# Quantised attention with keys on partitions, four heads in column groups, GpSimd rounding, and output written in parts

## The chip, the cores and the metric

The kernel runs on one core of a Trainium2 chip. The metric is device microseconds of one execution, and of several executions the median. A core has TensorE (PE in the rows; PEld is its weight load), VectorE (DVE), ScalarE (ACT), GpSimd (POOL), and the queue engine SP, which here issues nearly all transfers. They run side by side and wait for each other through semaphores. SBUF is the working memory of 128 partitions; PSUM has eight banks of 512 float32 columns by 128 partitions and takes TensorE's results.

## What is computed

The reference is four gated layers of cross-attention and feed-forward on x of shape (4, 512, 512), so 2048 rows of 512. The change lies in the attention of layer 1, over all 2048 rows as queries and all 2048 rows of the context as keys, with 16 heads of 32:

```
q = fq(LN(x) @ Wq + bq) per head and row;  k = fq(ctx @ Wk + bk) likewise   # fq: 8 bits, symmetric
v = fq(ctx @ Wv + bv) per column
s = q k^T / sqrt(32);  p = exp(s - max s)
p255 = round(255 p)            # 0 to 255
o = (p255 @ v) / sum(255 p)    # per head
x = x + tanh(g) * (o @ Wp + bp)
```

The mask of this layer leaves every key in.

## The kernel before

The program is a list of stages, one after the other, with a barrier of all engines between them. Each stage has its own semaphores and one instruction list for each engine. Layer 1's attention consists of split_weights, quantised_heads for the keys, quantised_values, split_weights, transposed_parts (which normalises x and turns it), quantised_heads for the queries, attention_quantised, split_weights of the output weights, transposed_parts of the attention's output, and project_and_add. A number "in parts" is stored as two float16 values, high and low, so that TensorE can multiply float32 data in float16 steps: in PARTS, high by high, low by high, high by low.

quantised_heads works on 16 tiles of 128 rows. TensorE projects a tile, VectorE adds the bias, takes each head's largest magnitude, scales and rounds, and TensorE turns the result, so that the head's 32 numbers lie on partitions. For the keys (L = 2) it multiplies the rounded numbers by their step again, and ScalarE and GpSimd split them in two parts. For the queries (L = 1) the rounded integers are turned as they are, and the steps go to sq, one for each row and head.

attention_quantised has queries on partitions. It works in 256 tiles: for each head, 16 tiles of 128 queries against all 2048 keys. A tile n goes through these steps:

- score_for_top: four products of 512 keys, of which VectorE takes the maximum each (L1616); top_of and shift_of make of them the shift of the exponential. This runs two tiles ahead.
- score: the same four products again into two pairs of banks, and ScalarE takes the exponential of each pair of banks (1024 keys, L1585), with the row's shift as bias and sq as scale. The result is written as int16, which rounds it, and the unrounded sum goes to z.
- turn: 16 transposes of 128x128 (L1516) bring keys to partitions. VectorE copies one half back as float16 (L1629), ScalarE the other (L1591).
- mix: 16 products of 128x128 by 128x32 (L1524), and VectorE moves the 32 columns to o (L1634).
- At a head's end GpSimd divides by the sums (L1495 to L1497).

The order is written out by hand in each engine's list (tile, head_from_tile_1). SP loads the queries and keys of head h + 3 into a ring of three once head h is scored. After the stage, transposed_parts splits o into high and low, turns it into oT, and project_and_add multiplies it.

Two other attentions of the program, attention_clipped (layer 2) and attention_causal (layer 3), already have keys on partitions, take the sums by a product with ones, and put four float32 products of 32 columns side by side in TensorE's column groups. Some rows below are theirs.

## Time and profile before

| | |
|---|---|
| median of 3 runs | 3445.23 us (3444.49 to 3451.05) |
| the profiled execution's own time | 3446.79 us |
| its span | 3445.1 us |
| TensorE busy | 2739.6 us, 80% |
| VectorE busy | 2552.2 us, 74% |
| ScalarE busy | 1874.1 us, 54% |
| GpSimd busy | 706.1 us, 20% |
| mean granted clock of TensorE | 0.897 of full speed |

The shares are means over all stages, which have different limits. Layer 1's attention_quantised begins at 872.95 us and ends at 1798.71 us, more than a quarter of the span. A busy time does not say what an engine waited for; that is read from the timeline, which lists each instruction, or each run of alike ones, with its start and its time.

### The profile page before, as it was taken

To read this page: it belongs to the slowest core of one execution; us is meant where nothing else is said; L and a number is where in the kernel's file an instruction comes from. 1 tells how busy PE (TensorE), PEld (TensorE's weight loads), DVE (VectorE), ACT (ScalarE), POOL (GpSimd) and SP (SyncE) were. 2 spreads that over 40 slices of the span, in tenths; PEclk is the share of its full clock that TensorE was granted. 3 is DMA by queue.
4 is the path that set the end of the run, shared out by engine and by line. 5 is a ranking of instruction groups with operands and counts; after the bars stand their busy time and mean duration, and the time that the engine had idled before them with its cause. 6 is when DMAs were issued, how large, how long until landed. Compare 5 with 4: busy or idle time off the path is not lost. (4 is left out here: it accounts for less than half of the span.)

```text
span 3445.1 us, 63421 instructions
## 1 busy us (share of the span) xinstructions
PE 2739.6 (80%) x21404; PEld 1417.0 (41%) x21404; DVE 2552.2 (74%) x4757; ACT 1874.1 (54%) x2709; POOL 706.1 (20%) x602
## 2 busy tenths in 40 slices
PE   5768999677799999999977777777797657759983
PEld 3344444233465656565644333334111323224542
DVE  5656677657899999999975666434798878986547
ACT  2564433232699999999982533313676313434541
POOL 4340000102110100101004233203012603550013
PEclk8978999887899999999999888887998869978996
DMA  4533421200100000000001000100431100022301
GB/s 150 182 127 123 147 74 37 83 0 16 25 7 13 7 13 7 13 7 13 1 13 63 26 0 0 61 15 13 98 74 37 59 0 0 0 83 50 66 8 52
DMA packets 65334, 151.93 MB, mean 44 GB/s; under 512 B 11840, under 2 KB 20048, under 8 KB 63376
## 3 DMA queue, kind: packets, MB, share of 16 engines
q1 hardware_dynamic: 62368, 140.43, 13.6%
q0 software_dynamic: 2800, 9.18, 0.8%
q8 instruction: 117, 1.92, 0.2%
q14 instruction: 49, 0.40, 0.0%
HBM read 93.61 MB, written 24.38 MB: 34 GB/s over the span
## 5 line engine op out<-in xcount | busy, mean ns | idle before, releaser
L1616 DVE TENSOR_REDUCE s_top<-ps 128x1 f32<-128x512 f32 x1024 | 656.2, 682 | 30.4 <-PE ps L1511 30.1
L1585 ACT ACTIVATE s_prob<-ps,s_shift,m_sq 128x1024 int16<-128x1024 f32 x512 | 615.3, 1202 | 30.9 <-DVE s_shift L1624 30.9
L1511 PE MATMUL ps<-s_ks,s_qs 128*128 128x512 f16 x1024 | 352.6, 386 | 61.7 <-issue 15.0
L1516 PEld LDWEIGHTS ps<-ident,s_prob 128*128 128x128 f16 x4096 | 272.7, 98 | 123.4 <-DVE m_o L1634 52.2
L1516 PE MATMUL ps<-ident,s_prob 128*128 128x128 f16 x4096 | 314.1, 220 | 0.7 <-ACT s_prob L1585 0.5
L1504 PE MATMUL ps<-s_ks,s_qs 128*128 128x512 f16 x1024 | 307.2, 382 | 0.8 <-ACT s_prob L1585 0.5
L1591 ACT ACTIVATE s_probT<-ps 128x1024 f16<-128x1024 int16 x256 | 262.1, 1024 | 6.2 <-PE ps L1516 5.8
L1007 PE MATMUL ps<-m_hT,m_w 128*128 128x512 f16 x1024 | 231.9, 381 | 1.8 <-PEq L104 1.8
L248 PE MATMUL ps<-ident,s_parts 128*128 128x128 f16 x640 | 76.4, 293 | 129.1 <-POOL s_parts L239 127.3
L1629 DVE CAST s_probT<-ps 128x1024 f16<-128x1024 int16 x256 | 174.0, 680 | 5.0 <-PE ps L1516 5.0
L2288 DVE TENSOR_SCALAR s_prob<-ps,s_cap 128x1024 f32<-128x1024 f32 x128 | 158.1, 1269 | 25.2 <-PE ps L2197 25.2
L1495 POOL TENSOR_TENSOR s_sums<-s_z 128x16 f32<-128x16 f32 x16 | 3.5, 218 | 835.3 <-DVE m_o L1634 835.3
L2897 DVE TENSOR_REDUCE s_ntop<-ps 128x1 f32<-128x512 f32 (+3 forms) x256 | 107.3, 482 | 86.6 <-PE ps L2757 86.6
L2232 ACT ACTIVATE s_prob<-s_prob 128x1024 f32<-128x1024 f32 x128 | 131.1, 1051 | 58.8 <-DVE s_prob L2288 55.8
L1058 ACT ACTIVATE s_silu<-ps,scale 128x512 f32<-128x512 f32 x64 | 43.9, 686 | 205.4 <-PE ps L1007 205.4
L1007 PEld LDWEIGHTS ps<-m_hT,m_w 128*128 128x128 f16 x1024 | 100.5, 98 | 124.0 <-issue 2.4
L1511 PEld LDWEIGHTS ps<-s_ks,s_qs 128*128 (+1 forms) x1024 | 80.1, 96 | 168.4 <-DVE s_top L1616 108.7
L2211 PE MATMUL ps<-s_prob,m_values 128*32 128x512 f32 x512 | 136.0, 610 | 12.8 <-ACT s_prob L2232 12.6
L1524 PE MATMUL ps<-s_hv,s_probT 128*128 128x32 f16 x4096 | 142.4, 177 | 1.7 <-ACT s_probT L1591 1.7
L2868 ACT ACTIVATE s_prob<-ps 128x384 f32<-128x384 f32 (+1 forms) x192 | 89.7, 516 | 88.2 <-PE ps L2780 87.9
L2214 PE MATMUL ps<-s_prob,s_ones 128*32 128x512 f32 x512 | 136.0, 610 | 0.0
L1524 PEld LDWEIGHTS ps<-s_hv,s_probT 128*128 128x128 f16 x4096 | 129.7, 96 | 2.2 <-issue 2.2
(402 smaller groups left out, 5844.3 us busy)
## 6 DMA issues: line engine op xcount, KB each, us to landing
s_qs<-m_qT SPq DMA_DIRECT2D x144, 128.0 KB, 3.1
s_ks<-m_kT SPq DMA_DIRECT2D x96, 128.0 KB
numbers<-s_numbers SPq DMA_DIRECT2D x21, 512.0 KB, 2.8
s_slabs<-numbers SPq DMA_DIRECT2D x21, 512.0 KB, 6.0
m_ks<-context_parts SPq DMA_DIRECT2D x12, 512.0 KB
expert_rows<-s_y SPq DMA_DIRECT2D x19, 256.0 KB, 2.0
s_rows_in<-in_ctx SPq DMA_DIRECT2D x16, 256.0 KB, 3.1
x_sb<-in_L_ffn_W_up SPq DMA_DIRECT2D x4, 1024.0 KB, 6.7
```

The lines of the kernel that those rows point to most:

```text
L1007: i = pe.matmul(k.ps[:, 2 * (n % 2) + j, :], wt[:, c, cols(n, P)], hT[:, l, c, cols(g, GT)], start=(l == c == 0), stop=(l == 1 and c == DC ...
L1504: j = pe.matmul(pair(half)[:, m, :], qs[:, hb, bass.ds(t * P, P)], ks[:, hb, cols(2 * half + m, 512)], start=True, stop=True)
L1511: pe.matmul(quarter_at(q), qs[:, hb, bass.ds(t * P, P)], ks[:, hb, cols(q, 512)], start=True, stop=True).then_inc(s.top_scored, 1)
L1516: j = pe.transpose(turned(half, F16)[:, cols(m, P)], prob[:, u, cols(8 * half + m, P)].bitcast(F16), k.ident[:])
L1524: j = pe.matmul(output, probT[:, u, m, :], hv[:, hb, m, :], start=(m == 0), stop=(m == T - 1))
L1585: act.activation(prob[:, u, cols(half, HALF)], pair(half).rearrange("p m n -> p (m n)"), ACT.Exp, bias=shift[:, u:u + 1], scale=sq[:, bass ...
L1591: act.activation(probT[:, u, 8:16, :].rearrange("p m n -> p (m n)"), turned(1, I16), ACT.Copy).then_inc(s.half1_copied, 1)
L1616: dve.tensor_reduce(top4[:, u, q:q + 1], quarter_at(q), AX.X, ALU.max).then_inc(s.top_read, 1)
L1629: dve.tensor_copy(probT[:, u, 0:8, :].rearrange("p m n -> p (m n)"), turned(0, I16)).then_inc(s.half0_copied, 1)
L2211: pe.matmul(values_at(m)[cols(j, HD), :], values[:, b * KT + t, 2 * pair + j, :], prob[:, n % R, j, :], start=(t == 0), stop=(t == KT - 1))
L2214: i = pe.matmul(sums_at(m)[cols(j, HD), :], ones[:], prob[:, n % R, j, :], start=(t == 0), stop=(t == KT - 1))
L2288: dve.tensor_scalar(prob[:, n % R, :, :], k.ps[:, 2 * (n % A):2 * (n % A) + 2, :], cap[:, tile:tile + 1], -LIMIT, ALU.min, ALU.max).then_i ...
```

## The change

attention_quantised is written anew, with keys on partitions. It works in 16 blocks of four heads (the four of one 128-partition group) by 512 queries; a block has 16 steps n, one for each tile of 128 keys.

- The queries come as two parts, already multiplied by their steps, as the keys do: quantised_heads is called with parts=qT, and sq is gone. Queries and keys are stacked three times in 96 rows (high by high, high by low, low by high), so a score is one product of 96 rows.
- top: as before, four products of 512 keys with 128 queries on partitions, and VectorE takes their maxima, now negated. It runs AHEAD = 19 steps ahead of the scores. Once a block, shifts makes of them 128x16 values in three float16 parts (five small instructions), turn_shift transposes these, copy_shift brings them to SBUF, and SP writes them to three further rows of the queries, rows 96 to 98, against which the keys have a constant in the same rows. The product of 99 rows then gives the score with the shift taken off.
- score: four products a step (one for each head) of 128 keys by 512 queries, in a ring of three banks. ScalarE takes the exponential of each bank by itself, as float32, with ln 255 as bias.
- GpSimd rounds the step's 128x2048 numbers into float16 integers (one instruction).
- mix_values, two steps late (LAG): four products of 32 columns, one for each head, in four column groups of one bank, integers by values in float16. mix_ones: the same with the unrounded float32 numbers and ones, for the sums, in another bank. Both accumulate over 16 steps.
- Once a block: ScalarE evacuates both banks (step 1 of the next block), pick_sums brings the sums' rows to partitions (step 5), VectorE inverts them, spread_inverse lays the inverses out (step 8), VectorE divides, ScalarE writes the high part, GpSimd the low part, straight into qT. project_and_add reads qT; the transposed_parts of the output is gone.
- In quantised_heads, the multiplication by scale is fused into the one by the inverse step.

The order of TensorE in a step is score 0, top 0, mix_values, score 1, top 1, mix_ones, score 2, top 2, score 3, top 3. The whole stage is written out without loops.

```diff
 def quantised_heads(k, src, w, bias, scale, sq=None, ints=None, parts=None, context=False):
...
-                    if scale != 1.0:
-                        v.done(dve.tensor_scalar(inv[:], inv[:], scale, None, ALU.mult))
-                    v.done(dve.tensor_tensor(scaled[:, u, :].rearrange("p (h d) -> p h d", d=HD),
-                                             rows[:, u, :].rearrange("p (h d) -> p h d", d=HD),
-                                             inv[:].unsqueeze(2).broadcast_to([P, H, HD]), ALU.mult))
+                    v.done(dve.scalar_tensor_tensor(scaled[:, u, :].rearrange("p (h d) -> p h d", d=HD),
+                                                    rows[:, u, :].rearrange("p (h d) -> p h d", d=HD), scale,
+                                                    inv[:].unsqueeze(2).broadcast_to([P, H, HD]), ALU.mult, ALU.mult))
...
-def attention_quantised(k, qT, sq, kT, values, o):
+def attention_quantised(k, qT, kT, values):
...
+            for b in range(BLOCKS):
+                sp.wait_ge(s.top_read, number["shift", b] + 1)
+                sp.dma_start(qs[ROWS:ROWS + 3, b % 3, :, :], shiftT[:, b % 2, :]).then_inc(shifted[b % 3], 16)
+                if b and b + 2 < BLOCKS:
+                    sp.wait_ge(s.scored, A * KT * b)
+                    for a in range(A):
+                        queries(b + 2, a, q_loaded[(b + 2) % 3])
+                if b and b % G == 0 and b // G + 1 < DC:
+                    for a in range(A):
+                        keys(b // G + 1, a, k_loaded[(b // G + 1) % 2])
...
+            for n in range(STEPS + KT):
+                if n < STEPS:
+                    pool.wait_ge(s.exp_ready, A * (n + 1))
+                    if n >= 3:
+                        pool.wait_ge(s.mixed, n - 2)
+                    pool.tensor_scalar(ints[:, n % 3, :, :], prob[:, n % 4, :, :], ROUND, ROUND, ALU.add,
+                                       ALU.subtract).then_inc(s.rounded, 1)
+                if n >= KT and n % KT == LOW:
+                    b = n // KT - 1
+                    at = (slice(None), 1, b // G, cols(b % G, GT))
+                    pool.wait_ge(s.hi_ready, b + 1)
+                    pool.tensor_tensor(qT[at], num[:], qT[:, 0, b // G, cols(b % G, GT)], ALU.subtract).then_inc(s.lo_ready, 1)
...
+            def bank_free(job):
+                if job >= 3:
+                    pe.wait_ge(s.top_read, job - 2)
...
+            def score(n, a):
+                b, t = n // KT, n % KT
+                g = A * n + a
+                if t == a == 0:
+                    pe.wait_ge(shifted[b % 3], 16 * (b // 3 + 1))
+                if g >= 3:
+                    pe.wait_ge(s.exp_ready, g - 2)
+                pe.matmul(score_at(g), ks[0:ROWS + 3, b // G % 2, a, cols(t, P)], qs[0:ROWS + 3, b % 3, a, :],
+                          start=True, stop=True).then_inc(s.scored, 1)
+
+            def mix_values(n):
+                b, t = n // KT, n % KT
+                if t == 0 and b:
+                    pe.wait_ge(s.evacuated, 2 * b)
+                pe.wait_ge(s.rounded, n + 1)
+                for a in range(A):
+                    pe.matmul(mixed_at[cols(a, HD), :], values[:, t, cols(b // G * A + a, HD)], ints[:, n % 3, a, :],
+                              start=(t == 0), stop=(t == KT - 1))
+
+            def mix_ones(n):
+                t = n % KT
+                for a in range(A):
+                    j = pe.matmul(sums_at[cols(a, HD), :], ones[:], prob[:, n % 4, a, :],
+                                  start=(t == 0), stop=(t == KT - 1))
                 j.then_inc(s.mixed, 1)
...
+            def pick_sums(b):
+                job = number["pick", b]
+                bank_free(job)
+                pe.wait_ge(s.evacuated, 2 * (b + 1))
+                for q in range(TG):
+                    j = pe.matmul(top_at(job)[:, cols(q, A)], sums[:, cols(q, P)], pick[:], start=True, stop=True)
+                j.then_inc(s.top_scored, 1)
+
+            def spread_inverse(b):
+                job = number["wide", b]
+                bank_free(job)
+                pe.wait_ge(s.top_read, number["pick", b] + 1)
+                for q in range(TG):
+                    for a in range(A):
+                        j = pe.matmul(top_at(job)[cols(a, HD), cols(q, P)],
+                                      inv[:, A * q + a:A * q + a + 1].broadcast_to([P, HD]), k.ident32[:],
+                                      start=True, stop=True)
+                j.then_inc(s.top_scored, 1)
+
+            for m in range(-AHEAD, END):
+                i = m + AHEAD
+                for a in range(A):
+                    if 0 <= m + 1 < STEPS:
...
+                        score(m + 1, a)
+                    if i < STEPS:
+                        top(i, a)
+                    if a == 0 and LAG <= m < STEPS + LAG:
+                        mix_values(m - LAG)
+                    if a == 1 and LAG <= m < STEPS + LAG:
+                        mix_ones(m - LAG)
+                if i % TILES == 0 and 0 < i <= STEPS:
+                    turn_shift(i // TILES - 1)
+                if m >= KT and m % KT == PICK:
+                    pick_sums(m // KT - 1)
+                if m >= KT and m % KT == WIDE:
+                    spread_inverse(m // KT - 1)
...
+            def exp(n, a):
+                g = A * n + a
+                if a == 0 and n >= 4:
+                    act.wait_ge(s.mixed, n - 3)
+                act.wait_ge(s.scored, g + 1)
+                act.activation(prob[:, n % 4, a, :], score_at(g), ACT.Exp, bias=ln255[:, 0:1]).then_inc(s.exp_ready, 1)
+
+            def evacuate(b):
+                if b:
+                    act.wait_ge(s.lo_ready, b)
+                act.wait_ge(s.mixed, KT * (b + 1))
+                act.activation(sums[:], sums_at, ACT.Copy).then_inc(s.evacuated, 1)
+                act.activation(num[:], mixed_at, ACT.Copy).then_inc(s.evacuated, 1)
...
+            def shifts(b):
+                dve.wait_ge(s.top_read, number["top", TILES * (b + 1) - 1, 3] + 1)
+                hi, mid, lo = (shift[:, b % 2, r, :] for r in range(3))
+                v.done(dve.tensor_reduce(least[:], ntop[:, b % 2, :, :], AX.X, ALU.min))
+                v.done(dve.tensor_scalar(hi, least[:], 1.0 / SIXTEEN, None, ALU.mult))
+                v.done(dve.scalar_tensor_tensor(rest[:], least[:], 1.0 / SIXTEEN, hi, ALU.mult, ALU.subtract))
+                v.done(dve.tensor_scalar(mid, rest[:], 1.0, None, ALU.mult))
+                dve.tensor_tensor(lo, rest[:], mid, ALU.subtract).then_inc(s.shift_ready, 1)
...
 def layer1_xattn(k):
...
-            quantised_heads(k, hT, wq, k.i.L1_xattn_bq, scale, sq=sq[:].rearrange("p (h t) -> p t h", t=T), ints=qT)
-        o = sb("o", [P, H, T, HD], F32)
-        attention_quantised(k, qT, sq, kT, values, o)
+            quantised_heads(k, hT, wq, k.i.L1_xattn_bq, scale, parts=qT)
+        attention_quantised(k, qT, kT, values)
...
-            transposed_parts(k, oT, tiles=o)
-            project_and_add(k, oT, wp, k.i.L1_xattn_bp, 1)
+            project_and_add(k, qT, wp, k.i.L1_xattn_bp, 1)
```

## Rows read from the trace of the kernel before

**Rows 1.** The page's costliest groups: the attention's maxima, exponentials and copies.

```profile
L1616 DVE TENSOR_REDUCE s_top<-ps 128x1 f32<-128x512 f32 x1024 | 656.2, 682 | 30.4 <-PE ps L1511 30.1
L1585 ACT ACTIVATE s_prob<-ps,s_shift,m_sq 128x1024 int16<-128x1024 f32 x512 | 615.3, 1202 | 30.9 <-DVE s_shift L1624 30.9
...
L1591 ACT ACTIVATE s_probT<-ps 128x1024 f16<-128x1024 int16 x256 | 262.1, 1024 | 6.2 <-PE ps L1516 5.8
```

**Rows 2.** Busy time by stretch: PE, PEld, DVE, ACT, POOL, then PE clock, DMA, GB/s.

```profile
896.00:1792.00 896.00, 846.83 (x10180) 542.42 (x10178) 865.98 (x2028) 875.57 (x1272) 71.16 (x59) 0.99 0.04 8
```

**Rows 3.** Timeline at the attention's ends: start us, us, engine, line, operation, count.

```profile
872.95 0.62 SPq L1473 DMA_DIRECT2D s_qs<-m_qT  x1
...
889.16 2.48 DVE L1616 TENSOR_REDUCE s_top<-ps 128x1 f32<-128x512 f32 x4 [1.00 <-PE ps L1511]
...
1797.66 1.05 POOL L1497 TENSOR_TENSOR m_o<-m_o,s_sums 128x512 f32<-128x512 f32 x1
...
1810.63 0.69 DVE L1216 TENSOR_TENSOR m_wp<-s_nat,m_wp 128x512 f16<-128x512 f32 x1 [0.58 <-ACT m_wp L1210]
...
1831.59 0.69 DVE L267 COPY m_oT<-ps 128x1024 f16<-128x1024 f16 x1 [0.41 <-PE ps L248]
```

**Rows 4.** Timeline of TensorE: a plain run, then a group in columns.

```profile
295.27 3.62 PE L1007 MATMUL ps<-m_hT,m_w 128*128 128x512 f16 x16
...
2499.78 0.38 PE L2197 MATMUL ps<-s_qs,s_ks 128*128 128x512 f16 x1
...
2500.09 0.62 PE L2211 MATMUL ps<-s_prob,m_values 128*32 128x512 f32 x2
...
2500.55 0.60 PE L2211 MATMUL ps<-s_prob,m_values 128*32 128x512 f32 x2
...
2501.09 0.60 PE L2197 MATMUL ps<-s_qs,s_ks 128*128 128x512 f16 x2
```

**Rows 5.** Timeline of the causal attention: picking of sums, exponentials, evacuation.

```profile
3155.06 1.00 PE L2802 MATMUL ps<-s_pick,s_sums 128*128 128x4 f32 x8
...
3199.85 0.57 ACT L2868 ACTIVATE s_prob<-ps 128x512 f32<-128x512 f32 x1
...
3204.65 0.59 ACT L2876 ACTIVATE s_sums<-ps 64x512 f32<-64x512 f32 x1 [0.23 <-PE ps L2791]
...
3205.92 1.05 ACT L2868 ACTIVATE s_prob<-ps 128x512 f32<-128x512 f32 x2
```

**Rows 6.** Groups of GpSimd by shape: busy us, mean ns of one, idle before.

```profile
L2273 POOL TENSOR_TENSOR s_out<-s_num,s_inv 128x512 f32<-128x512 f32 x16 | 20.3, 1270 | 126.2 <-DVE s_inv L2296 126.2
...
L1487 POOL COPY s_hv<-m_values 128x512 f16<-128x512 f16 x16 | 9.7, 611 | 1.0
...
L1495 POOL TENSOR_TENSOR s_sums<-s_z 128x16 f32<-128x16 f32 x16 | 3.5, 218 | 835.3 <-DVE m_o L1634 835.3
...
L141 POOL CAST ident<-ident 128x128 f16<-128x128 f32 x1 | 0.3, 291 | 0.1
```

**Rows 7.** The page's DMA issues: KB of one, median us from issue to landing.

```profile
s_qs<-m_qT SPq DMA_DIRECT2D x144, 128.0 KB, 3.1
```

**Rows 8.** Timeline of quantised_heads: of the keys, then of the queries.

```profile
643.85 4.44 PE L1246 MATMUL ps<-m_wkv,m_cT 128*128 128x512 f16 x13 [21.86 <-PEq L104]
...
707.07 1.15 POOL L1318 TENSOR_TENSOR s_f<-s_rows,s_f 128x512 f16<-128x512 f32 x1 [2.97 <-ACT s_f L1330]
707.68 0.57 DVE L1290 TENSOR_SCALAR s_step<-s_amax 128x16 f32<-128x16 f32 x1
...
717.59 1.02 ACT L1339 ACTIVATE m_kT<-ps 128x1024 f16<-128x1024 f16 x1 [1.44 <-PE ps L1254]
...
811.08 8.12 PE L1246 MATMUL ps<-m_wq,m_hT 128*128 128x512 f16 x30 [1.69 <-PEq L104]
...
816.79 0.17 DVE L1290 TENSOR_SCALAR s_step<-s_amax 128x16 f32<-128x16 f32 x1
...
871.63 0.60 ACT L1335 ACTIVATE m_qT<-ps 128x512 f16<-128x512 f16 x1 [3.00 <-PE ps L1254]
```

335 lines of the change are left out of this document (142 added, 193 removed).

## The prediction

> **What bounds the kernel now.** I first read the page's costliest groups [rows 1] to find where the touched function stands, then the busy times of its long stretch [rows 2], then the timeline at its two ends [rows 3]. From 896 to 1792 us ScalarE is busy 875.6 of 896 us (98%), VectorE 97%, TensorE 95% and GpSimd 8%. Why ScalarE: each of the 256 tiles (16 heads by 16 query tiles) asks it for two exponentials of 1202 ns and one copy of 1024 ns, 3.43 us [rows 1], and 256 of these are 878 us. VectorE is just behind with four maxima and a copy. The reader should see that three engines are nearly full: relief for one only hands the end to the next. The stage starts with SP's first transfer at 872.95 and ends with GpSimd's product at 1798.71 [rows 3]: 925.8 us. All other stages stand before or behind it, so the sum is over stages, each with its own bound.
>
> **The new step.** There are again 256 steps (16 blocks of four heads by 512 queries, 16 key tiles each). A step has on TensorE four score and four top products of 512 columns, a group of four value products in float16 and a group of four ones products in float32. On ScalarE four exponentials, on VectorE four maxima, on GpSimd one rounding of 128x2048.
>
> TensorE. A 512-column product costs 0.216: sixteen take 3.62, less one duration 0.38, by 15 [rows 4]. Eight are 1.73. The ones group is priced by the attention that already packs four float32 products in column groups of 32: the last plain product starts at 2499.78, the group at 2500.09, its second passes at 2500.55, the next plain product at 2501.09 [rows 4]. That is 1.31 us from plain to plain, less the 0.216 of the plain one: 1.10, of which two passes are 0.92 and about 0.18 is going in (0.09) and out (0.08). The trace has no float16 group in columns. Bounds: 0.22, if one pass is all it costs, and 0.86, if its four products follow each other. I take one pass (0.216), the 0.04 by which four starts are staggered, and the same in and out, 0.44, since the float32 rows show both. Step: 1.73 + 1.10 + 0.44 = 3.27 us.
>
> The Trainium skill, TensorEngine Tiling (Array Packing), Key Properties, says that changing the tiling mode drains TensorE; the float32 rows agree with 0.09 in and 0.08 out. This speaks against the change, because the order of the step changes mode four times; without that rule's cost the step would be about 2.9 us, the first rival below.
>
> VectorE. Four maxima take 2.48 back to back, the last one's tail included [rows 3]: 0.60 apart, 2.40 a step. ScalarE. Two exponentials of 128x512 take 1.05, each 0.57: 0.48 apart [rows 5], 1.92 a step. Both lie beside TensorE's 3.27. I checked the rings by these numbers: the score three back has been read some 0.5 us or more before its bank is wanted, and the top three back likewise.
>
> GpSimd. No row shows this rounding. One-input rows: 128 columns cost 291 ns, 512 cost 611 [rows 6], so 0.83 ns a column, and 2048 are 1.9 us. Two-input rows: 16 columns 218 ns, 512 columns 1270, so 2.12 ns, and 2048 are 4.5 us. The rounding has one input and two constants, so I take 1.9, hidden under 3.27; 4.5 is kept for the range. It has two steps of slack before the value products need it. The Trainium skill, GPSIMD Engine Reference, Elementwise, side-by-side cycle accounting, puts a body of up to two operations at 1.03 cycles an element, an estimated 1.8 us, but also names about 1.8 cycles as a best case, an estimated 3.1; no row here tells them apart.
>
> **Sum over the new stage.**
> - Start: six transfers issued at 0.62 each before the first top [rows 3], a landing of 3.1 [rows 7], the first product: 7.5.
> - Lead-in: tops run 19 steps ahead, and the value products start two steps late, so 21 steps go at VectorE's 2.40: 50.4, plus the first shift chain of 1.5 (five small dependent instructions, 0.3 each): 51.9. TensorE may fall to 1.2 GHz here; its four products would be 1.7, still under 2.40. This is new: before, tops were two tiles ahead.
> - 235 full steps at 3.27: 768.5.
> - The last 18 steps have no tops: 4 x 0.216 + 1.10 + 0.44 = 2.40, 43.2, with one block's extra 3.6; then three steps of 1.53: 51.4.
> - Tail: two copies (1.2), pick (0.95), reciprocal, spread (1.1), division, high part, low part (1.2): about 7.2.
> - Once a block on the path, 14 times inside the full steps: pick_sums, eight instructions in 1.00, of which 0.95 hold the next [rows 5]; spread_inverse, 16 float32 products of 128 columns four at a time, 4 x 2 x 0.11 + 0.18 = 1.1; and the evacuation. ScalarE waits for the block's last ones group, ending 2.5 us into the step, with the next four exponentials queued behind the wait. The two copies (0.59 each [rows 5]) put the first of these at 3.65; its bank is wanted for the fourth score at 2.84 and is free at about 4.45 (0.57 of the exponential, and an estimated 0.2 to the release): a stall of 1.6. Together 3.65 x 14 = 51.
> - The shift chain, 15 times. VectorE's own slack is 0.87 a step. But GpSimd rounds while it runs, and a small VectorE instruction between SBUF tiles waits for a GpSimd instruction: 0.57 us under GpSimd's product, 0.17 without it [rows 8]. The rounding runs from about 0.7 to 2.65 of a step and the chain starts at 1.05, so it is held to 2.65 and ends near 3.8. The next four maxima wait behind it, and TensorE, three banks ahead, waits for the first of them: 1.9, plus 0.1 for the shift's transpose, 2.0 x 15 = 30. Bounds: 0.4 if nothing holds it, 8 if each of its four such instructions waits a whole rounding.
>
> Sum: 7.5 + 51.9 + 768.5 + 51.4 + 7.2 + 51 + 30 = 967.5 against 925.8: +41.7.
>
> **Transfers.** The queue SP issues twelve query transfers a block (7.5 us) and waits for scores. By the order written out, the next queries have 14 steps (45 us) and the shift rows two steps (6.5 us, 4.8 in the lead-in) against an issue of 0.62 and a landing of about 3. I cost them at nothing; without that cover a late shift is some 2 us a block.
>
> **The stages around it.** The queries' quantised_heads now writes two parts, as the keys' does: keys 643.85 to 718.61, queries 811.08 to 872.23 [rows 8], 74.8 against 61.2, so +13.6. The fused multiplication changes nothing for the keys, whose scale is 1. Dropping the transposed_parts of the output takes its stage away, from 1811.32 to 1832.28 [rows 3]: -21.0. Total: 41.7 + 13.6 - 21.0 = +34.3. The profiled execution took 3446.79, 1.6 above the median of 3445.23, so the forecast is 3481.1 for such an execution and 3480 for a median. Measurement can tell 0.2% (6.9 us) from no change.
>
> **Rivals.**
> - Faster: the changes of mode cost nothing and the float16 group one pass. Step 1.73 + 0.22 + 0.92 = 2.87; 253 steps by 0.40 are 101 us: 3379. For it: no row shows a float16 group, and weight loads elsewhere hide under products. Against: 2500.09 and 2501.09. It decides once the step is under 3.27 - 41.2/253 = 3.11; a half-way case lands at 3430. Chance 0.20.
> - GpSimd takes about 3.2 us, half-way between its two rates. The low part (1.2 a block) is no longer hidden, the last 18 steps go at 3.3 instead of 2.4, and the chain is held longer: 17 + 16 + 15, 3530. Chance 0.15. The Trainium skill's 1.8 cycles on the page named above would be this case.
> - GpSimd at the two-input rate: 256 x 4.6 + 16 x 1.2 + 65 = 1262, +336 in the stage: 3774. Chance 0.05. It decides above 3.3 us a rounding.
> - The locks take the full 8 us a block: 6 x 15 = 90 more: 3570. Chance 0.08.
> - The forecast, TensorE bound near 3.27 with stalls of 2 to 6 us a block: 0.52, its own range 3443 to 3510.
>
> Faster takes the first rival and a sliver of the forecast's low side, 0.22; within 0.2% another 0.12 of that low side, where the evacuation and the chain hide; slower the rest, 0.66. The range 3425 to 3560 reaches into the first rival and over the second and leaves out about 0.2.
>
> **What would show it.** TensorE near full in the stage at 3.27 us a step, VectorE near 75%, ScalarE near 60%, GpSimd near 60%; a rounding of 1.9 us; 0.44 between plain products around the float16 group; one gap of 1.6 us a block waiting for an exponential and one of about 2 for a maximum; 45 us of maxima alone at the start; the queries' stage 13 us longer, the output's 21 us gone. Wrong would be: a step under 3.11, or GpSimd as the releaser of the value products.

## The result, and the profile after

The changed kernel takes 4413.09 us (median of four, 4412.75 to 4417.90), against 3444.86 for the kernel before beside it: a ratio of 1.2815, with a 95% interval of 1.2799 to 1.2831. It is 968 us slower. The forecast was 3480, with a range to 3560: the direction was right and the size was not.

The page's costliest groups of the changed kernel (busy us, mean ns of one, then the idle time before them and what ended it); they answer to [rows 1]:

```profile
L1519 POOL TENSOR_SCALAR s_ints<-s_prob 128x2048 f16<-128x2048 f32 x256 | 1808.8, 7087 | 56.8 <-ACT s_prob L1628 56.8
L1660 DVE TENSOR_REDUCE s_ntop<-ps 128x1 f32<-128x512 f32 x1024 | 669.0, 687 | 867.9 <-PE ps L1544 865.6
L1628 ACT ACTIVATE s_prob<-ps,s_ln 128x512 f32<-128x512 f32 x1024 | 665.0, 687 | 1084.4 <-PE ps L1561 1082.1
...
L1570 PE MATMUL ps<-s_ints,m_values 128*32 128x512 f16 x1024 | 129.6, 496 | 443.1 <-POOL s_ints L1519 443.1
```

One group stands out. GpSimd's rounding takes 7.087 us, 256 times, and has no idle time but the lead-in's 56.8 us. The value products have waited 443 us, all of it for that rounding: the sign that the forecast named last, GpSimd as their releaser. The busy times of a long stretch say the same (us, then PE, PEld, DVE, ACT, POOL, PE clock, DMA share, GB/s), to be held against [rows 2]:

```profile
1000.00:1700.00 700.00, 486.70 (x2219) 112.25 (x2216) 341.55 (x441) 265.14 (x411) 700.00 (x105) 0.72 0.03 6
```

GpSimd is busy 700.00 of 700 us, no other engine more than 70%. TensorE's granted clock is 0.72 here, against 0.99 in [rows 2]. The timeline at the stage's two ends, to be held against [rows 3]:

```profile
887.31 2.67 SPq L1478 DMA_DIRECT2D s_qs<-m_qT  x3
...
2776.95 0.62 PE L1570 MATMUL ps<-s_ints,m_values 128*32 128x512 f16 x4 [4.74 <-POOL s_ints L1519]
...
2786.35 1.15 POOL L1525 TENSOR_TENSOR m_qT<-s_num,m_qT 128x512 f16<-128x512 f32 x1 [9.45 <-ACT m_qT L1639]
...
2799.88 0.33 SPq L1711 DMA_DIRECT2D s_bias_bc<-in_L_xattn_bp  x1
```

The stage runs from 887.31 to 2787.50, 1900.2 us against 925.8: +974.4. It begins 14.4 us later than before, for the queries' longer stage. After the output's weights the projection follows at once, so the stage of transposed parts with its 21.0 us is gone. Together +967.8, against 971.1 between the two profiled spans (4416.2 and 3445.1). The stage is told in one line: 55.4 to the first rounding (942.75), 256 roundings 7.07 apart (1810), fifteen low parts of 1.16 between them in the same queue (17.4), some 7 of gaps, and 10.6 behind the last rounding, which ends at 2776.9 (the sixteenth low part is in it).

Two side effects stand in the timeline of the middle:

```profile
1470.02 49.47 POOL L1519 TENSOR_SCALAR s_ints<-s_prob 128x2048 f16<-128x2048 f32 x7
...
1477.17 0.62 PE L1570 MATMUL ps<-s_ints,m_values 128*32 128x512 f16 x4 [3.42 <-POOL s_ints L1519]
...
1484.24 4.44 DVE L1668 SCALAR_TENSOR_TENSOR s_rest<-s_least,s_shift 128x16 f32<-128x16 f32 x1
...
1488.71 2.56 DVE L1669 TENSOR_SCALAR s_shift<-s_rest 128x16 f16<-128x16 f32 x1
...
1496.40 0.61 PE L1544 MATMUL ps<-s_ks,s_qs 96*128 96x512 f16 x1 [9.48 <-DVE s_ntop L1660]
```

TensorE waits 3.42 us for the rounding, and its next group of four takes 0.62 instead of 0.40, at the lower of its two clocks (1.2 GHz). VectorE's small instructions of 128x16, 0.17 us where nothing holds them, take 4.44 and 2.56, because a rounding holds them. The roundings start 7.07 apart, at 1477.09, 1484.16 and 1491.23. The first of the two, with two tensors as input, comes free 4.5 us into a rounding and not at its end; the second, with one, starts there and is held to the end. The chain of the shift takes over 12 us this way, and TensorE waits 9.48 for a maximum behind it. This costs nothing here, since GpSimd never runs dry of work meanwhile.

### The profile page after: what moved, and what is told of

Same layout as the page of the kernel before. It is cut to its first block and busy times, and to the rows that moved or that the text cites. A ratio compares the mean times of both kernels' runs of the same rounds, so it can differ in the third digit from the quotient of the medians.

```text
span 4416.2 us, 48145 instructions
## 1 busy us (share of the span) xinstructions
PE 3163.0 (72%) x16876; PEld 1160.9 (26%) x16876; DVE 2568.3 (58%) x3829; ACT 1687.2 (38%) x2501; POOL 2454.1 (56%) x812
## 3 DMA queue, kind: packets, MB, share of 16 engines
q8 instruction: 117, 1.92, 0.2%
## 5 line engine op out<-in xcount | busy, mean ns | idle before, releaser
L1519 POOL TENSOR_SCALAR s_ints<-s_prob 128x2048 f16<-128x2048 f32 x256 | 1808.8, 7087 | 56.8 <-ACT s_prob L1628 56.8
L1660 DVE TENSOR_REDUCE s_ntop<-ps 128x1 f32<-128x512 f32 x1024 | 669.0, 687 | 867.9 <-PE ps L1544 865.6
L1628 ACT ACTIVATE s_prob<-ps,s_ln 128x512 f32<-128x512 f32 x1024 | 665.0, 687 | 1084.4 <-PE ps L1561 1082.1
L1544 PE MATMUL ps<-s_ks,s_qs 96*128 96x512 f16 x1024 | 503.7, 494 | 134.2 <-DVE s_ntop L1660 125.7
L1561 PE MATMUL ps<-s_qs,s_ks 99*128 99x512 f16 x1024 | 497.5, 491 | 16.1 <-ACT s_prob L1628 15.0
L1570 PE MATMUL ps<-s_ints,m_values 128*32 128x512 f16 x1024 | 129.6, 496 | 443.1 <-POOL s_ints L1519 443.1
L1576 PE MATMUL ps<-s_prob,s_ones 128*32 128x512 f32 x2048 | 422.3, 911 | 0.0
L1561 PEld LDWEIGHTS ps<-s_qs,s_ks 99*128 99x128 f16 x1024 | 112.7, 111 | 558.7 <-issue 407.5
L1544 PEld LDWEIGHTS ps<-s_ks,s_qs 96*128 96x128 f16 x1024 | 113.9, 111 | 256.9 <-DVE s_ntop L1660 172.3
L2629 POOL TENSOR_TENSOR s_summed<-s_y,s_bits 128x512 f32<-128x512 f32 x64 | 104.2, 1629 | 71.3 <-DVE s_bits L2659 71.3
L2249 PE MATMUL ps<-s_prob,s_ones 128*32 128x512 f32 x512 | 135.2, 607 | 0.0
```

The costliest lines, as they stand in the source:

```text
L1519: pool.tensor_scalar(ints[:, n % 3, :, :], prob[:, n % 4, :, :], ROUND, ROUND, ALU.add, ALU.subtract).then_inc(s.rounded, 1)
L1544: pe.matmul(top_at(job), qs[0:ROWS, b % 3, a, cols(tile, P)], ks[0:ROWS, c % 2, a, cols(q, GT)], start=True, stop=True).then_inc(s.top_sco ...
L1561: pe.matmul(score_at(g), ks[0:ROWS + 3, b // G % 2, a, cols(t, P)], qs[0:ROWS + 3, b % 3, a, :], start=True, stop=True).then_inc(s.scored, 1)
L1570: pe.matmul(mixed_at[cols(a, HD), :], values[:, t, cols(b // G * A + a, HD)], ints[:, n % 3, a, :], start=(t == 0), stop=(t == KT - 1))
L1576: j = pe.matmul(sums_at[cols(a, HD), :], ones[:], prob[:, n % 4, a, :], start=(t == 0), stop=(t == KT - 1))
L1628: act.activation(prob[:, n % 4, a, :], score_at(g), ACT.Exp, bias=ln255[:, 0:1]).then_inc(s.exp_ready, 1)
```

## The experiments

Each starts from the changed kernel. Times are medians, ratios are against the kernel before on the same chip.

**1. GpSimd's operations by themselves.** A stage of its own, ahead of the attention, runs each operation three times, each waiting for the one before:

```diff
+    v.done(pool.tensor_scalar(b16[:], a32[:], ROUND, ROUND, ALU.add, ALU.subtract))      # L1434
+    v.done(pool.tensor_scalar(b16[:, 0:512], a32[:, 0:512], ROUND, ROUND, ALU.add, ALU.subtract))
+    v.done(pool.tensor_scalar(b16[:], a32[:], 1536.0, None, ALU.add))
+    v.done(pool.tensor_scalar(b32[:], a32[:], ROUND, ROUND, ALU.add, ALU.subtract))
+    v.done(pool.tensor_copy(b16[:], a32[:]))
+    v.done(pool.tensor_tensor(b32[:], a32[:], a32[:], ALU.add))
+    v.done(pool.tensor_scalar(b16[:], a16[:], ROUND, ROUND, ALU.add, ALU.subtract))      # L1446
```

The rounding was then repeated beside a busy VectorE (maxima, then roundings) and a busy ScalarE, and at last VectorE's own forms were run alone.

> The changed kernel with a stage of its own ahead of the attention, in which single operations run one after the other, each waiting for the one before; output unchanged. In the changed kernel GpSimd's rounding (two operations, float32 to float16, 128x2048) took 7.09 us, against 1.9 in the forecast. Theory A: that is GpSimd's own rate for this form, so it takes about 7.0 us (3.4 ns a column) with all other engines idle, and no less with VectorE or ScalarE busy beside it; 512 columns then take about 1.9. Theory B: contention (memory ports shared with VectorE, or with all) makes it slow: alone it takes 2 to 4.5 us, and 7 only beside a busy VectorE. Theory C: each arithmetic operation costs: the form with one operation takes about half, 3.5. Theory D: the float16 output costs: float32 to float32 is far below 7. The same operation on VectorE is expected at 1.2 us for float32 input (the nearest row of the kernel before has 1.23 for 128x2048) and 0.6 to 1.2 for float16 input.

The groups of that stage by shape (busy us, mean ns of one, idle before):

```profile
L1434 POOL TENSOR_SCALAR s_b<-s_a 128x2048 f16<-128x2048 f32 x3 | 21.3, 7102 | 0.3
L1440 POOL TENSOR_SCALAR s_b<-s_a 128x2048 f32<-128x2048 f32 x3 | 21.3, 7087 | 0.2
L1446 POOL TENSOR_SCALAR s_b<-s_a 128x2048 f16<-128x2048 f16 x3 | 21.3, 7085 | 0.3
L1438 POOL TENSOR_SCALAR s_b<-s_a 128x2048 f16<-128x2048 f32 x3 | 16.1, 5365 | 0.2
L1444 POOL TENSOR_TENSOR s_b<-s_a 128x2048 f32<-128x2048 f32 x3 | 10.8, 3597 | 0.2
...
L1436 POOL TENSOR_SCALAR s_b<-s_a 128x512 f16<-128x512 f32 x3 | 5.8, 1922 | 0.2
L1442 POOL CAST s_b<-s_a 128x2048 f16<-128x2048 f32 x3 | 5.7, 1891 | 0.2
```

With every other engine idle the rounding takes 7.10 us. It is GpSimd's own rate for this form, 3.46 ns a column, whatever the types. Theory A holds; B (contention) and D (the float16 output) fall. C is half right: with one operation instead of two it takes 5.37, three quarters and not half. A plain copy of the same 2048 columns takes 1.89, and an addition of two tensors 3.60. So the forecast's 1.9 us was the right price for a copy, and not for a copy with arithmetic: an operation with a constant costs 3.5 us over the copy, and the second one 1.7 more.

The same line beside busy engines, and VectorE's rounding beside it (durations are min/median/max):

```profile
L1450 POOL TENSOR_SCALAR s_b<-s_a x9: 7085/7086/8063, 990.2 to 1055.3; 128x2048 f16<-128x2048 f32 x9
```

```profile
L1464 DVE TENSOR_SCALAR s_c<-s_a x12: 1226/1227/7989, 1039.0 to 1073.1; 128x2048 f16<-128x2048 f32 x12
```

Maxima or ScalarE's copies beside it change nothing (7.09). VectorE's rounding does collide: alone 1.23 us, beside GpSimd's up to 7.99, since one waits for the other. The three VectorE roundings of 7.98 to 7.99 each end 1.1 us behind GpSimd's instruction, and GpSimd's three beside them take 7.93 to 8.06 instead of 7.09. The Trainium skill, SBUF — State Buffer, "SBUF: two separate sides", states an exclusive lock on the pair of ports for a whole instruction. The 7.99 agree with it. The 4.44 above don't: there a small instruction came free 4.5 us into a rounding of 7.09, so it is not always the whole instruction. From float16, VectorE's rounding takes 0.69.

**2. A quarter of the rounding.**

```diff
-  pool.tensor_scalar(ints[:, n % 3, :, :], prob[:, n % 4, :, :], ROUND, ROUND, ...
+  pool.tensor_scalar(ints[:, n % 3, 0, :], prob[:, n % 4, 0, :], ROUND, ROUND, ...
...
-  pe.matmul(mixed_at[cols(a, HD), :], values[:, t, cols(b // G * A + a, HD)], ints[:, n % 3, a, :],
+  pe.matmul(mixed_at[cols(a, HD), :], values[:, t, cols(b // G * A + a, HD)], ints[:, n % 3, 0, :],
```

> GpSimd rounds only the first of the four heads (128x512), and the value products of all four read that one tile: three quarters of the rounding are left out, all other work stays. Theory (the forecast with one wrong price): a rounding costs by its columns, 7.09 / 4 = 1.8 us, GpSimd leaves the path, TensorE bounds at 3.27 us a step and the time is the forecast's, 3480 (3440 to 3510). Rival 1: the 7 us are mostly a fixed cost or contention, the rounding stays above 3.3 and the time above 3550. Rival 2: the forecast's other terms were also too low (mode changes, evacuation, shift chain, the clock), then 3520 to 3600 with a rounding of 1.8. Rival 3: mode changes cost less than 0.18 a group: below 3440.

It took 3477.06 us, a ratio of 1.0096 (1.0079 to 1.0112). The forecast for the whole change was 3480. With the rounding at the price that the forecast gave it, the rest of the sum comes out. Its stage, from the timeline:

```profile
883.21 2.84 SPq L1478 DMA_DIRECT2D s_qs<-m_qT  x3
...
1849.05 1.15 POOL L1525 TENSOR_TENSOR m_qT<-s_num,m_qT 128x512 f16<-128x512 f32 x1 [7.98 <-ACT m_qT L1639]
```

That is 967.0 us, where the sum said 967.5. How much of that is luck is seen in its steps:

```profile
1092.83 1.92 POOL L1519 TENSOR_SCALAR s_ints<-s_prob 128x512 f16<-128x512 f32 x1 [1.35 <-ACT s_prob L1628]
...
1093.51 0.17 DVE L1668 SCALAR_TENSOR_TENSOR s_rest<-s_least,s_shift 128x16 f32<-128x16 f32 x1
...
1166.38 0.39 PE L1561 MATMUL ps<-s_qs,s_ks 99*128 99x512 f16 x1 [1.30 <-ACT s_prob L1628]
...
1168.37 1.93 PE L1576 MATMUL ps<-s_prob,s_ones 128*32 128x512 f32 x8
...
1175.66 0.40 PE L1570 MATMUL ps<-s_ints,m_values 128*32 128x512 f16 x4
1175.99 0.39 PE L1561 MATMUL ps<-s_qs,s_ks 99*128 99x512 f16 x1
1176.22 0.38 PE L1544 MATMUL ps<-s_ks,s_qs 96*128 96x512 f16 x1
1176.53 1.06 PE L1576 MATMUL ps<-s_prob,s_ones 128*32 128x512 f32 x8
1177.53 0.39 PE L1561 MATMUL ps<-s_qs,s_ks 99*128 99x512 f16 x1
...
1178.94 0.40 PE L1570 MATMUL ps<-s_ints,m_values 128*32 128x512 f16 x4
```

From values group to values group are 3.28 us, against 3.27 in the sum. The stall for the evacuation is 1.30, and the whole step with it is 4.88 us, 1.6 over a plain one, as in the sum. Behind it the clock falls for one ones group (1.93 instead of 1.06) and four products; blocks in which it does so are 58.08 us apart, those without it 56.50. The chain of the shift costs TensorE 0.5 (that step is 3.80), where the sum had 2.0. Its four small arithmetic instructions stood inside a running rounding of 1.92 us, as the sum had it, and still took 0.17 to 0.19 each: none was held. So the block's 57.97 was right as a whole with two wrong parts: 2.0 for a lock that held nothing here, and nothing for a clock that cost 1.6.

**3. Half of the rounding**, the first edit above with `0:2` for `0`; the value products read `ints[:, n % 3, a % 2, :]`.

> GpSimd rounds two of the four heads (128x1024); the value products of the other two read the same tiles: half of the rounding is left out. Theory (GpSimd bounds once a rounding is over 3.3 us): by the rows of 512 columns (1.92) and 2048 (7.09) it takes 3.65; 256 x 3.66 + 58 lead-in + 16 x 1.16 for the low parts + 10 tail = 1024 in the stage, 98 more than before, less 7 around it: 3536 (3520 to 3560). Rival: TensorE's own step and stalls at a lower clock add to it, since it now waits for GpSimd in every step: 3600 and more.

3511.12 us, 1.0199 (1.0182 to 1.0216), 9 below the range given. A rounding takes 3.63, as expected. GpSimd is busy without a gap and TensorE nearly so, as the busy times show (columns as above):

```profile
1000.00:1600.00 600.00, 571.16 (x3684) 159.90 (x3688) 436.08 (x735) 421.72 (x687) 600.00 (x174) 0.99 0.05 13
```

The two engines' blocks are nearly equal: blocks are 58.64 us apart, GpSimd's full queue, where TensorE alone took 56.50 or 58.08 in run 2. The forecast's "decides above 3.3 us" compared GpSimd with a bare step; with the block's own stalls in TensorE's account it decides above (56.5 - 1.16) / 16 = 3.46 or (58.1 - 1.16) / 16 = 3.56, an estimate from run 2's two kinds of block.

**4. VectorE rounds**, all four heads, behind its maxima.

```diff
+            def round(n):
+                dve.wait_ge(s.exp_ready, A * (n + 1))
+                if n >= 3:
+                    dve.wait_ge(s.mixed, n - 2)
+                dve.tensor_scalar(ints[:, n % 3, :, :], prob[:, n % 4, :, :], ROUND, ROUND, ALU.add,
+                                  ALU.subtract).then_inc(s.rounded, 1)
...
                 if i < STEPS:
                     tops(i)
+                if 0 <= m < STEPS:
+                    round(m)
```

> All work is done, but the rounding moves from GpSimd to VectorE, behind the four maxima of its step. Theory: VectorE takes 2.40 + 1.23 = 3.63 us a step and becomes the bound, 235 steps of 3.63 instead of 3.27, no lock on the shift chain, some 2 us of small VectorE instructions a block on the path: 3515 (3490 to 3550). Rival 1: the rounding on VectorE is as slow as on GpSimd, 7 us: above 4900. Rival 2: VectorE gets it at half the columns' time (0.7 us), then TensorE bounds and it is 3450 to 3480.

3531.0 us, 1.0255 (1.0238 to 1.0272), within the range. VectorE is the bound at 3.52 us a step (1193.51 to 1197.03; 3.8 on a block's mean), the rounding 1.22:

```profile
1193.51 1.22 DVE L1677 TENSOR_SCALAR s_ints<-s_prob 128x2048 f16<-128x2048 f32 x1
1194.64 2.47 DVE L1654 TENSOR_REDUCE s_ntop<-ps 128x1 f32<-128x512 f32 x4
1197.03 1.22 DVE L1677 TENSOR_SCALAR s_ints<-s_prob 128x2048 f16<-128x2048 f32 x1
```

Moving one operation to another engine wins back 882 of the 968 us, with all the work done.

**5. GpSimd copies instead of computing.** The copy converts to int16, and this conversion stands in for the rounding; no run compares its integers one by one with those of the two operations. TensorE reads the bits of the integer n as the float16 n x 2^-24.

```diff
-        ints = s.sb("ints", [P, 3, A, GT], F16)
+        ints = s.sb("ints", [P, 3, A, GT], I16)
...
-  pool.tensor_scalar(ints[:, n % 3, :, :], prob[:, n % 4, :, :], ROUND, ROUND, ALU.add, ALU.subtract)
+  pool.tensor_copy(ints[:, n % 3, :, :], prob[:, n % 4, :, :])
...
-  pe.matmul(mixed_at[...], values[...], ints[:, n % 3, a, :], ...
+  pe.matmul(mixed_at[...], values[...], ints[:, n % 3, a, :].bitcast(F16), ...
...
-  act.activation(num[:], mixed_at, ACT.Copy)
+  act.activation(num[:], mixed_at, ACT.Copy, scale=float(2 ** 24))
```

> All work is done, but GpSimd no longer adds and subtracts the rounding constant: it copies the float32 probabilities to int16, whose conversion rounds, and the value products read the integers' bits as float16, where n is n times 2 to the minus 24; the evacuation of the values multiplies by 2 to the 24. By the measurement alone a GpSimd copy of 128x2048 takes 1.89 us, against 7.1 for the two operations. Theory (only the price of the rounding was wrong): the step is TensorE's 3.27 us and the time that of the kernel which rounds a quarter, 3477 (3465 to 3490). Rival 1: the conversion to int16 is not at the copy's rate and GpSimd bounds again: above 3600. Rival 2: TensorE is slower on such bits: 3500 and more.

3491.33 us, 1.0142 (1.0125 to 1.0159), one above its range. The copy takes 1.893 us in place:

```profile
L1519 POOL CAST s_ints<-s_prob 128x2048 int16<-128x2048 f32 x191 | 361.6, 1893 | 328.9 <-ACT s_prob L1627 328.9
```

Most of the 14 us over the run with a quarter of the rounding are TensorE's waits for a maximum behind the shift chain, 0.86 us in each block (from 1000 to 1700 us: us in total, times, longest):

```profile
PE ps L1560 <- ACT s_prob L1627: 14.4, 11, 1.3
PE ps L1543 <- DVE s_ntop L1659: 10.3, 12, 0.9
```

The copy, unlike run 2's rounding, holds the chain's first small instruction to its own end: 1.46 us instead of 0.17, in every block. This is the whole change with only the price of the rounding put right: it still isn't faster than the kernel before.

**6. Both column groups together**, with a quarter of the rounding, as in run 2.

```diff
-                    if a == 1 and LAG <= m < STEPS + LAG:
+                    if a == 0 and LAG <= m < STEPS + LAG:
                         mix_ones(m - LAG)
```

> GpSimd rounds a quarter (three quarters of the rounding are left out), as in the first timed run, and the ones group follows the values group at once instead of two plain products later, so that TensorE goes into column groups and out of them once a step and not twice. Theory of the forecast: going in and out costs 0.18 each time, 253 x 0.18 = 45 less: 3432 (3420 to 3445). Rival 1: changes of mode are free and the group's time is its own: 3477. Rival 2: with both groups together the score ring stalls (1.5 us without a score, ScalarE has two banks in hand), so that the gain is lost: 3460 to 3500.

3406.56 us, 0.9897 (0.9881 to 0.9914), better than its range: 70 less than run 2, where 45 were expected. The step, from one values group to the next:

```profile
1122.06 0.40 PE L1570 MATMUL ps<-s_ints,m_values 128*32 128x512 f16 x4
1122.29 1.03 PE L1576 MATMUL ps<-s_prob,s_ones 128*32 128x512 f32 x8
1123.25 0.39 PE L1561 MATMUL ps<-s_qs,s_ks 99*128 99x512 f16 x1
...
1125.10 0.40 PE L1570 MATMUL ps<-s_ints,m_values 128*32 128x512 f16 x4
```

3.04 us instead of 3.28: one way out of the column groups and one way in, 0.24. Times 253 that is 61, an estimate. Counted by blocks, they are 52.94 apart against 56.50 in run 2 where its clock stays up: 3.6 less, with a shorter stall at the evacuation (0.87 instead of 1.30, as the ones are done sooner) and somewhat longer steps around the shift. The 1.6 of low clock that eleven of run 2's blocks had besides are gone: the clock is 1.00 from 950 to 1750 us. 15 x 3.6 + 11 x 1.6 = 71. The Trainium skill, TensorEngine Tiling (Array Packing), Key Properties, says that a change of the tiling mode drains TensorE; the 0.24 agree with it.

**7. Runs 5 and 6 together**, all work done, sums from unrounded float32.

> All work is done: GpSimd copies to int16, probabilities and ones stay float32, and the ones group follows the values group at once. Theory: the order saves what it saved with a quarter of the rounding (3477 to 3407, 70), so the run with the copy to int16, 3491, becomes 3421 (3410 to 3435), 0.7% under the kernel before. Rival: the longer GpSimd instruction and VectorE's shift chain behind it cost the gain: 3445 or more.

3430.62 us, 0.9970 (0.9959 to 0.9980): within its range, 0.3% faster than the kernel before. The small instruction of the shift chain is held again (L1666 took 1.44 us in the blocks read, 0.17 where nothing holds it), and TensorE waits 1.24 for a maximum behind it.

**8. Float16 probabilities and ones**, added to run 5, so that the ones group is one pass.

```diff
-        prob = s.sb("prob", [P, 4, A, GT], F32)
+        prob = s.sb("prob", [P, 4, A, GT], F16)
...
-        ones = s.sb("ones", [P, HD], F32)
+        ones = s.sb("ones", [P, HD], F16)
```

> As the run with the copy to int16, and the probabilities and the ones are float16 (the sums are then of probabilities rounded to float16), so that the ones group is one pass. Theory: TensorE's step is 1.73 + 0.44 + 0.44 = 2.61 us, 0.66 less on 235 steps and on the last 18, 167 less than 3477, and with VectorE only 0.2 below TensorE its small instructions cost some 15 more: 3325 (3300 to 3350). Rival 1: a float16 group in columns costs near the float32 one when it reads float16 written by ScalarE, no gain: 3470. Rival 2: VectorE or the evacuation bounds at 2.9 or more a step: 3390 and more.

3510.39 us, 1.0191 (1.0126 to 1.0257). Its executions scatter more than any other's, from 3489.58 to 3553.12, the longer the lower their mean clock; the profiled one took 3492.92. So it is no faster than run 5, and whether it is slower is open. None of the three mechanisms explains it. Where TensorE has its full clock the step is 2.61 us, as the theory said (1403.06 to 1405.67). But its mean clock is 0.77:

```profile
1000.00:1600.00 600.00, 570.47 (x2972) 165.72 (x2970) 449.36 (x721) 421.09 (x671) 314.47 (x171) 0.77 0.05 13
```

The timeline where it falls:

```profile
1145.58 0.39 PE L1543 MATMUL ps<-s_ks,s_qs 96*128 96x512 f16 x1 [1.52 <-DVE s_ntop L1659]
...
1146.34 0.55 PE L1560 MATMUL ps<-s_qs,s_ks 99*128 99x512 f16 x1
1146.77 0.61 PE L1543 MATMUL ps<-s_ks,s_qs 96*128 96x512 f16 x1
```

A wait of 1.52 us, and a product of 512 columns then takes 0.61 and starts 0.43 after the last, down from 0.38 and 0.22. At that clock a step is 4.74 us, TensorE is busy but for one wait of 0.86, and still the clock came back only at 1177.27, 31 us later.

**9. The same with VectorE rounding** (run 4 with the edit of run 8).

> VectorE rounds, as in the second run, but from float16 probabilities, with float16 ones. By the measurement alone the rounding then takes 0.69 us instead of 1.23. Theory: VectorE bounds at 2.40 + 0.70 = 3.10 us a step instead of 3.63: 238 x 0.53 = 126 less than 3531, 3405 (3390 to 3425). Rival: the cost of the small instructions and waits a step is more than that sum, 3430 to 3450.

3592.81 us, 1.0448 (1.0426 to 1.0469), slower than with float32 by 62. VectorE's rounding is indeed 0.686 instead of 1.22, yet TensorE's clock is 0.74 from 1000 to 1600, where run 4 had 0.98 from 1000 to 1700. An estimate of the balance: from 955 to 1955 us the mean clock is 0.73, so it is low for some 540 us; steps take 4.73 there instead of about 3.1, so some 114 steps lose 1.6 each, 185 us, against the 126 that the cheaper rounding was to save.

**10. Runs 7 and 8 together**: GpSimd copies, float16 probabilities and ones, both groups in one.

> All work is done: GpSimd copies to int16, probabilities and ones are float16, and the ones group follows the values group at once. At the full clock the step is 2.61 - 0.18 = 2.43 us on TensorE and 2.40 on VectorE. Theory (a wait for VectorE's maximum behind the shift chain, 1.5 us once a block, is followed by TensorE's half clock, as in the run with float16 ones apart): the clock still falls, and it is that run's 3510 less 45: 3465 (3420 to 3500). Rival: the clock fell because the groups left TensorE too little work, and with them together it stays up: 3260 (3240 to 3300).

3310.9 us, 0.9615 (0.9599 to 0.9631), the fastest so far, 131 us under the kernel before. Its sums are of probabilities rounded to float16. The theory was too dark, the clock is 0.95 and not near 0.77, though the wait a block is longer than in run 8 (1.88 for 1.52):

```profile
1000.00:1600.00 600.00, 560.47 (x3813) 188.07 (x3815) 545.88 (x926) 515.49 (x862) 402.82 (x218) 0.95 0.06 14
```

The rival was 50 us too low. Once a block GpSimd's copy holds the chain of the shift, and TensorE stands:

```profile
1202.52 1.89 POOL L1519 CAST s_ints<-s_prob 128x2048 int16<-128x2048 f16 x1 [0.50 <-ACT s_prob L1627]
...
1203.01 1.43 DVE L1666 TENSOR_SCALAR s_shift<-s_least 128x16 f16<-128x16 f32 x1
...
1205.73 0.39 PE L1543 MATMUL ps<-s_ks,s_qs 96*128 96x512 f16 x1 [1.88 <-DVE s_ntop L1659]
```

The copy began at 1202.52 and ended at 1204.41; the instruction of 128x16 behind it could not end before that. This is the lock of the forecast's chain step, at about its price, in a kernel whose step leaves VectorE no slack.

**11. The shift chain spread over a step**: run 10, with one small instruction behind each maximum of the next tile.

```diff
-    AHEAD = KT + 3
+    AHEAD = KT + 4
...
                     dve.tensor_reduce(ntop[:, b % 2, i % TILES, q:q + 1], top_at(job), ...)
+                    if chain:
+                        chain.pop(0)()
...
-                if i % TILES == TILES - 1 and i < STEPS:
-                    shifts(i // TILES)
```

> As the run with float16 probabilities and both groups together, and the five small instructions of the shift chain stand one behind each of the next step's maxima, with the tops one step further ahead, so that TensorE does not wait 1.5 us for a maximum once a block. Theory (it is that wait that brings the half clock): the clock stays near full and the time is 3260 (3240 to 3310). Rival 1: the clock falls all the same, after the waits for exponentials at the block's evacuation: 3400 and more. Rival 2: it gains only the wait, 15 x 1.5 = 22 us, against the run without the change.

3324.88 us, 0.9662 (0.9646 to 0.9678), 14 slower than run 10. The edit doesn't do what it was for. A single small instruction is enough to be held a whole copy, and the maxima queue behind it:

```profile
1253.63 1.88 DVE L1677 SCALAR_TENSOR_TENSOR s_rest<-s_least,s_shift 128x16 f32<-128x16 f32 x1
...
1256.17 0.39 PE L1543 MATMUL ps<-s_ks,s_qs 96*128 96x512 f16 x1 [1.69 <-DVE s_ntop L1659]
```

The wait of 1.7 us stays, and the clock falls once behind each of them: all 13 in this stretch, and no fall anywhere else. So the theory's question was not answered by this run, and asks for one without the wait.

**12. The shift chain on GpSimd**: run 10, with VectorE keeping only the minimum over the tiles. The other five instructions stand between two of GpSimd's copies, where nothing of GpSimd can hold them.

```diff
-    AHEAD = KT + 3
+    AHEAD = KT + 4
...
+            def shifts(b):                                   # GpSimd's
+                hi, mid, lo = (shift[:, b % 2, r, :] for r in range(3))
+                pool.wait_ge(s.least_ready, b + 1)
+                v.done(pool.tensor_scalar(scaled[:], least[:], 1.0 / SIXTEEN, None, ALU.mult))
+                v.done(pool.tensor_copy(hi, scaled[:]))
+                v.done(pool.tensor_tensor(rest[:], scaled[:], hi, ALU.subtract))
+                v.done(pool.tensor_copy(mid, rest[:]))
+                pool.tensor_tensor(lo, rest[:], mid, ALU.subtract).then_inc(s.shift_ready, 1)
...
+                if n < STEPS and n % KT == KT - 4 and n // KT + 1 < BLOCKS:
+                    shifts(n // KT + 1)
```

> As the fastest run so far (GpSimd copies to int16, float16 probabilities and ones, both groups together, 3311), but GpSimd itself does the small instructions of the shift chain between two of its copies, so that no small VectorE instruction can be held by a copy; only the minimum over the block's tiles stays on VectorE; tops run one step further ahead. Theory (the waits of 1.9 us for a maximum, once a block, are what TensorE's clock falls behind): they go, 15 x 1.9 = 28, and with them the low clock, some 5 us of it a block at half speed, 2.2 lost each time, 30 in all; one step more of lead-in costs 2.4: 3255 (3240 to 3275), clock 0.99 in the stage. Rival 1: the clock falls all the same, only the waits go: 3285, clock 0.95. Rival 2: five more instructions a block on GpSimd, 1.5 us, make its copies late, TensorE waits for them instead: 3300 and more.

3263.83 us, 0.9487 (0.9471 to 0.9503), within its range: 47 less than run 10 and 5.1% under the kernel before, with its sums too from float16. The stretch's busy times and clock, and TensorE's waits there (us in total, times, longest):

```profile
1000.00:1600.00 600.00, 575.91 (x4088) 196.12 (x4086) 536.82 (x905) 553.85 (x932) 449.49 (x307) 1.00 0.06 15
```

```profile
PE ps L1576 <- ACT s_prob L1643: 14.5, 25, 1.2
PE ps L1576 <- DMA s_qs<-s_shiftT: 8.5, 14, 0.6
```

No wait for a maximum is left, and the granted clock is 1.00 instead of 0.95. The VectorE instruction that stays, the minimum, takes 0.22 us in every block, as it did inside the roundings of the changed kernel. In this kernel the wait behind VectorE's held chain was what the clock fell behind; the step more of lead is not what did it, since run 11 has it too. Of the 47 us the chain's waits are about two thirds and the clock the rest: a block of run 10 without a fall takes 45.57, its mean block 46.65, a block here 43.38. What is next is seen too: the shift's transfer comes 0.6 us late in each block.

## Why the forecast was right in direction and wrong in size

**The step that failed** is the price of GpSimd: "The rounding has one input and two constants, so I take 1.9, hidden under 3.27; 4.5 is kept for the range." It measured 7.09 us. Both bounds were below it, because they came from rows of other operations [rows 6]: copies, and operations on two tensors. Run 1 shows that the number of inputs isn't what orders them (copy 1.89, two tensors 3.60, one constant 5.37, two constants 7.09). The Trainium skill, GPSIMD Engine Reference, Elementwise, side-by-side cycle accounting, gave an estimated 1.8 us for up to two operations, or 3.1 by its best case; the 7.09 measured here decide against both. The mechanism was among the rivals, "GpSimd at the two-input rate", with its place right and its chance put at 0.05; its sum with the measured price, 256 x 7.07 + 16 x 1.16 + 65 = 1893, is the stage's 1900.

**TensorE's step** held: 3.28 against 3.27 (run 2), and the values group is 0.42 for the 0.44 taken: in run 2 the plain product before it starts 0.31 earlier (0.22 its own, 0.09 going in), and the next starts 0.33 behind the group's start. The faster rival, changes of mode for nothing, falls: run 6 measured 0.24 for one way in and one out.

**VectorE and ScalarE beside it** held: hidden at 3.27. VectorE bounds where the rounding was put on it (run 4), and where TensorE's step is cheapest (runs 10 and 12, 2.40 us a step, its four maxima).

**The block's extras**, 3.65 + 2.0, were right in sum (58.08 measured against 57.97) and wrong in two parts that cancelled by luck: the chain 0.5 for 2.0, and 1.6 of low clock that the forecast didn't have. The evacuation's 1.6 came out, though not by its own working: for its 0.2 us to the release no row stood, and in run 2 the product starts 0.05 behind the exponential's end. The lock behind the chain is real, but not what the forecast took it for, a hold to the end of any GpSimd instruction: 4.44 us in the changed kernel, where it is hidden; nothing in run 2, inside a rounding of 1.92; and 1.4 to 1.9, to the copy's end, in runs 5, 7, 8, 10 and 11, where it costs. Run 12, in which no small arithmetic instruction is left on VectorE, has none of these waits. Why a rounding lets go early and a copy does not was not tested.

**The transfers** were hidden, as said: in run 2 TensorE's products waited for the shift's transfer once, 1.1 us before the first block, and its weight loads 3.8 us in 15 others together. In two other runs it is late in every block: 0.9 us in run 4, whose step is longer, and 0.6 in run 12, whose step is shorter.

**The stages around it**: the queries' stage +14.4 for 13.6, the output's gone for the 21.0.

So run 2 answers what the forecast would have been worth with the right price: 3477 against 3480, and run 5, with all the work done, 3491. Nothing else in it needed to be wrong for an error of 933 us.

What stays open is the rule by which TensorE's clock falls. In the stretches read, each fall comes within some 4 us of one of the block's waits, and in run 6, where the longest wait a block was 0.87 us, none came. The length of the wait alone doesn't decide: in run 5 the clock fell 2 us behind a wait of 0.86 in some blocks (1039.66) and not in others, a wait of 1.88 was passed at full clock in two blocks of run 10 (at 1113.89 and 1205.73), and run 10 waits longer than run 8 with a clock of 0.95 against 0.77. The two differ in the order of the groups, and no run tells why that helps. The clock stayed low for 3 to 10 us in runs 2 and 11 and for 6 to 57 in run 8. Run 12 shows that taking the wait away keeps it up, not how it is decided.

## What to carry to other kernels

An operation that no row shows needs its own measurement before it is given to an engine, above all to one that has no row with constants; bounds from other operations are not bounds. On this GpSimd a copy that converts takes 1.89 us, where two arithmetic operations take 7.09. Where an engine is fed in blocks, compare the others with its block, stalls included, and not with its bare step. And before a saving on TensorE is booked as time, look at its waits and its granted clock: here small VectorE instructions beside a full GpSimd queue were better put into that queue (run 12).

## What the runs showed of the hardware that I had not expected

- GpSimd, 128x2048, alone: copy with conversion 1.89 us, two tensors 3.60 (the same tile twice), one constant 5.37, two constants 7.09; the types don't matter for the last.
- A GpSimd copy of 1.89 us holds a small VectorE instruction to its end (1.46 in run 5). A rounding with two constants of 128x512 held none (0.17 to 0.19 in run 2); one of 128x2048 let an instruction with two input tensors go 4.5 us into its 7.09 and held one with a single input to the end.
- TensorE takes the bits of GpSimd's int16 integers as float16 values of n x 2^-24 at its usual rate: 393 ns a product in run 5, 390 in run 2.
- A cheaper step on TensorE can bring nothing in time: a step of 2.61 us at full clock took 3490 us at the least (run 8), one of 3.28 took 3491 (run 5), because the clock was 0.77 of full on the mean, with the engine busy 95% of the time; 47 us came back from taking one wait of 1.9 us a block out of a later version, some 16 of them from the clock.
